# Four staging slots stored from ScalarE's queue, one scatter per four gathers, tile numbers loaded four at a time: a four-layer graph network on one Trainium2 core

## The reference

```python
edge_index = jnp.stack([src, dst])
h = jnp.maximum(_layernorm(x, axis=-1), 0.0)
x = x + _L0_gnn_ref(h, edge_index, ...)      # and in the same way L1, L2, L3

# L0: a message per edge, batch norm over all edges, two segment sums, a two-layer MLP with batch norms
messages = jnp.concatenate([node_rep[src], edge_rep[dst]], axis=-1)
messages = _bn_relu(messages @ W1, g1, b1)
edge_new = jax.ops.segment_sum(messages, dst, num_segments=edge_rep.shape[0])
aggregate = jax.ops.segment_sum(edge_new[dst], src, num_segments=node_rep.shape[0])
h = (1.0 + epsilon) * node_rep + aggregate
out = _bn_relu(_bn_relu(h @ W2a, g2a, b2a) @ W2b, g2b, b2b)
# L1: norm = dinv[row] * edge_weight * dinv[col]; three times
agg = segment_sum(out[row] * norm[:, None], col)
out = out + relu(((1.0 - ALPHA) * agg + ALPHA * x0) @ conv_w[li])
# L2: attention over 4 heads for edge n < 3125, softmax over the heads
# L3: att = sigmoid(a1[row] + a2[col]); out = segment_sum(att[:, None] * x0_j[col], row)
```

## Time and profile before

| | |
|---|---|
| median of three runs | 3692.08 us (3691.84 to 3708.81) |
| the profiled execution | 3690.83 us, its span 3688.8 us |
| mean granted TensorE clock | 0.79 of full speed |
| TensorE (matmuls) / VectorE / ScalarE / GpSimd busy | 69% / 62% / 39% / 30% of the span |
| DMA | 632.29 MB, mean 171 GB/s |
| gather stage, by GpSimd's gathers (L806) | first at 562.0 us, last at 1308.7 us |
| message stage, by VectorE's adds (L1734) | first at 1357.8 us, last at 1751.3 us |
| agg0, by the transposes (L1168) | first at 1785.8 us, last at 2296.6 us |

### The profile page before, as it was taken

How to read it: one execution, slowest core, us unless ns; L and a number is a source line. 1 busy time by engine, 2 the same in 40 slices (tenths; PEclk the granted TensorE clock), 3 DMA queues, 4 the chain that set the end, 5 groups by cost and what they waited for, 6 DMA issues and landing times.

```text
span 3688.8 us, 41851 instructions
## 1 busy us (share of the span) xinstructions
PE 2561.8 (69%) x12402; PEld 2077.5 (56%) x12402; DVE 2288.3 (62%) x4379; ACT 1451.6 (39%) x3050; POOL 1099.4 (30%) x878
## 2 busy tenths in 40 slices
PE   4678714555555536666477777979999999925998
PEld 3522203554555524454366666459888988924786
DVE  4979926888888887877322222354565576626776
ACT  2278813444454410000233333544433434423765
POOL 0016776666666666777200000000000000051000
PEclk9788855555555558888698888979999999967999
DMA  9982225666666655554587777006546645340887
GB/s 373 378 307 27 26 21 155 176 182 184 188 186 188 185 128 141 138 136 105 159 257 230 240 238 216 26 26 185 171 127 172 194 125 169 114 99 8 300 313 265
DMA packets 332245, 632.29 MB, mean 171 GB/s; under 512 B 93155, under 2 KB 206556, under 8 KB 325372
## 3 DMA queue, kind: packets, MB, share of 16 engines
q1 hardware_dynamic: 240350, 550.88, 45.9%
q0 software_dynamic: 78464, 58.39, 10.4%
q10 hardware_dynamic: 13214, 20.35, 1.6%
HBM read 443.97 MB, written 185.52 MB: 171 GB/s over the span
## 4 chain that ended last, share of the span: by engine, by line
PE 31%; DMA 8%; DVE 6%; issue 3%; ACT 3%; SPq 1%; POOL 1%; another core or an unknown queue 0%; DVEq 0%; ACTq 0%
PE banks L1196 25%; DMA weights<-reg 6%; PE banks L1141 2%; DMA ring<-pairs 2%; PE banks L1168 2%; PE banks L1120 1%; ACT reg L996 1%; POOL pairs L798 1%; SPq L712 0%; ACT reg L860 0%; DVE reg L1943 0%; DVE stats L1412 0%; ACT reg L1021 0%; DVE lhs_r L1742 0%; DVE reg L1435 0%
## 5 line engine op out<-in xcount | busy, mean ns | idle before, releaser
L1196 PE MATMUL banks<-rows_r,lhs_r 128*128 128x448 f32 x3850 | 1037.9, 391 | 48.0 <-DVE wts L1853 10.9
L1196 PEld LDWEIGHTS banks<-rows_r,lhs_r 128*128 128x128 f32 x3850 | 756.1, 201 | 135.0 <-DVE att_low L601 23.9
L798 POOL DMA_INDIRECT pairs<-wts x391 | 626.3, 1602 | 501.4 <-DMA weights<-ring 258.5
L1284 PE MATMUL banks<-lhs_r,oT 128*128 x416 | 203.5, 489 | 424.9 <-issue 329.8
L603 DVE SCALAR_TENSOR_TENSOR ring_r<-ring,dinv,rows_r 128x896 fp32r<-128x896 f32 (+1 forms) x300 | 303.4, 1033 | 302.9 <-ACT rows_r L589 302.8
L806 POOL DMA_INDIRECT reg<-tab_p,w x416 | 402.5, 968 | 244.9 <-issue 146.2
L836 POOL DMA_INDIRECT el<-tab_l,base_i x25 | 24.8, 991 | 1481.7 <-DMA tab_l<-reg 1474.4
L589 ACT ACTIVATE rows_r<-ring,dinv 128x896 fp32r<-128x896 f32 (+1 forms) x300 | 284.6, 950 | 393.0 <-PE banks L1196 376.1
L1284 PEld LDWEIGHTS banks<-lhs_r,oT 128*128 128x128 f32 x416 | 132.8, 319 | 437.5 <-issue 437.3
L1323 PE MATMUL banks<-reg 128*128 128x256 f32 x832 | 252.5, 471 | 146.2 <-DVE reg L1734 139.4
L599 DVE TENSOR_TENSOR rows_r<-ring,rows_r 128x448 fp32r<-128x448 f32 x175 | 108.7, 625 | 394.1 <-ACT rows_r L585 394.1
(11 more groups left out here) (256 smaller groups left out, 4432.4 us busy)
## 6 DMA issues: line engine op xcount, KB each, us to landing
ring<-weights SPq DMA_DIRECT2D x225, 448.0 KB, 3.4
ring<-pairs SPq DMA_DIRECT2D x200, 448.0 KB, 4.8
pairs<-ring SPq DMA_DIRECT2D x25, 3136.0 KB, 25.6
ring<-pairs SPq DMA_DIRECT2D x75, 896.0 KB, 5.5
zbuf<-reg SPq DMA_DIRECT2D x208, 256.0 KB
reg<-zbuf SPq DMA_DIRECT2D x52, 1024.0 KB
weights<-reg SPq DMA_DIRECT2D x84, 384.0 KB, 4.8
ring<-weights SPq DMA_DIRECT2D x75, 224.0 KB, 3.3
```

Source lines behind the costliest of these rows:

```text
L798: pool.indirect_dma_start(pairs, bass.IndirectOffsetOnAxis(ap=ix_c[:, k:k + 1], axis=0), vals[:, k, :], None, compute_op=ALU.add).then_inc ...
L1196: m = pe.matmul(bank[:, 0:BLK], lhs[part], rows[:, c:c + BLK], start=first, stop=last)
L1284: m = pe.matmul(ps[4 + q % 2][:, k % 2 * H:(k % 2 + 1) * H], oT[q // 4 % 2][:, k % 8 * P:(k % 8 + 1) * P], part[:, bass.ds(tiles[k], 1), : ...
```

## The change

Three edits:

- **agg0.** `turned` has four slots in place of two; the two new ones lie in the room of `conv` and of `w1`, which are free by then. The stores are issued by ScalarE, one unit after the copy that fills the slot, and no longer by SyncE. The loads of `conv` and of the two attention vectors move behind a wait for all stores.
- **Scatters.** One scatter follows every fourth gather (`C_EVERY = 4`): 104 in the gather stage in place of 52, and 154 after it in place of 206.
- **Tile numbers.** TensorE and VectorE load four with one instruction. TensorE loads the eight of the next pass after the second of its four steps, VectorE where it did before.

```diff
-C_EVERY = 8
-TURN_LAG = 1
+C_EVERY = 4
 TURN_LEAD = 2
+TURN = 4
...
-        turned = [view(RF + k * 8 * P, 4, 2 * P) for k in range(2)]
...
+        turned = [view(RF, 4, 2 * P), view(RF + 8 * P, 4, 2 * P), weight(CONV, 4, 2 * P),
+                  w1_flat.rearrange("p (a b) -> p a b", a=4)]
...
         def turn_slot(q):
-            return pair_no[q] % 2
+            return pair_no[q] % TURN
...
             def stream(pi):
                 if pi == 1:
+                    wait_turned(sp)
+                    sp.dma_start(attn[:, 0, :], attn_l.rearrange("h d -> (h d)").unsqueeze(0).to_broadcast([P, H])).then_inc(gat_loaded, 16)
+                    sp.dma_start(attn[:, 1, :], attn_r.rearrange("h d -> (h d)").unsqueeze(0).to_broadcast([P, H])).then_inc(gat_loaded, 16)
                     sp.dma_start(conv[:, :, :], conv_w.rearrange("l (j p) n -> p (l j) n", p=P)).then_inc(conv_loaded, 16)
-                    wait_turned(sp)
                 for q in range(FIRST[pi] + (RING if pi == 0 else 0), FIRST[pi + 1]):
                     load_unit(q)
-                    if pi == 0 and q >= RING + TURN_LAG:
-                        store_turned(q - RING - TURN_LAG)
-                if pi == 0:
-                    for q in range(FIRST[1] - RING - TURN_LAG, FIRST[1]):
-                        store_turned(q)
...
                 if t % 2 == 0:
-                    wait(act, turn_stored[k], 32 * (pair_no[q] // 2))
+                    wait(act, turn_stored[k], 32 * (pair_no[q] // TURN))
...
+            def store_turned(q):
+
+                _, _, t, (b,) = UNITS[q]
+                if t % 2 == 0 and t < NT - 1:
+                    return
+                k, c0 = turn_slot(q), t // 2 * 2 * P
+                n = min(2 * P, LD - c0)
+                act.wait_ge(drained_a, nth[number["turn", (q,)]])
+                act.dma_start(weights_rows[b * BLK:b * BLK + 3 * P, c0:c0 + n].rearrange("(i p) c -> p i c", p=P),
+                             turned[k][:, 0:3, 0:n]).then_inc(turn_stored[k], 16)
+                act.dma_start(weights_rows[b * BLK + 3 * P:(b + 1) * BLK, c0:c0 + n],
+                             turned[k][0:BLK - 3 * P, 3, 0:n]).then_inc(turn_stored[k], 16)
+
             for q in range(FIRST[1]):
                 if q % ROWS == 0 and q // ROWS < NSPLIT:
                     high_step(0, q // ROWS)
                 high_rows(q)
+                if q > TURN_LEAD:
+                    store_turned(q - TURN_LEAD - 1)
                 if q >= TURN_LEAD:
                     turn_out(q - TURN_LEAD)
...
+            def load_tiles(i):
+
+                for k in range(8 * i, 8 * i + 8, 4):
+                    tiles[k:k + 4] = nc.values_load_multi_w_load_instructions(
+                        tile_ix[0:1, k:k + 4], engines=[pe.engine], min_val=0, max_val=NT - 1)[1]
...
                 if q % 4 == 0:
                     pe.wait_ge(oT_ready, q // 4 + 1)
-                    tiles[2 * q:2 * q + 8] = [pe.value_load(tile_ix[0:1, k:k + 1], min_val=0, max_val=NT - 1) for k in range(2 * q, 2 * q + 8)]
...
                     add_q(q)
+                    if q % 4 == 1 and i + 1 < NPASS:
+                        load_tiles(i + 1)
...
-                tiles = [v.value_load(tile_ix[0:1, k:k + 1], min_val=0, max_val=NT - 1) for k in range(8 * i, 8 * i + 8)]
+                tiles = []
+                for k in range(8 * i, 8 * i + 8, 4):
+                    tiles += nc.values_load_multi_w_load_instructions(
+                        tile_ix[0:1, k:k + 4], engines=[v.engine], min_val=0, max_val=NT - 1)[1]
```

More of the change, by code:

```diff
@@ L393, in gnn_kernel @@
         assert 10 * NCH <= CONV
+        turned = [view(RF, 4, 2 * P), view(RF + 8 * P, 4, 2 * P), weight(CONV, 4, 2 * P),
+                  w1_flat.rearrange("p (a b) -> p a b", a=4)]
+        assert len(turned) == TURN
         ix_c = wts[:, CONV:CONV + NCH].bitcast(I32)
@@ L450, in gnn_kernel @@
         same_ready, same_tot, cells_ready = names("same_ready", "same_tot", "cells_ready")
-        turn_stored = [sem(f"turn_stored{k}") for k in range(2)]
+        turn_stored = [sem(f"turn_stored{k}") for k in range(TURN)]
         pair_full = [sem(f"pair_full{k}") for k in range(RING // 2)]
@@ L540, in turn_slot @@
         def turn_slot(q):
-            return pair_no[q] % 2
+            return pair_no[q] % TURN
         def wait_turned(eng):
-            for k in range(2):
-                eng.wait_ge(turn_stored[k], 32 * len(range(k, n_pairs, 2)))
+            for k in range(TURN):
+                eng.wait_ge(turn_stored[k], 32 * len(range(k, n_pairs, TURN)))
         lhs_r = {at: rounded(f"lhs_r{at // W_}", at, W_) for at in sorted({at for pair in lhs_at for at in pair})}
@@ L702, in load_unit @@
                     sp.dma_start(slot[:, 0:n], weights_rows[t * P:(t + 1) * P, c0:c0 + n]).then_inc(full, 16)
-            def store_turned(q):
-                _, _, t, (b,) = UNITS[q]
-                if t % 2 == 0 and t < NT - 1:
-                    return
-                k, c0 = turn_slot(q), t // 2 * 2 * P
-                n = min(2 * P, LD - c0)
-                sp.wait_ge(drained_a, nth[number["turn", (q,)]])
-                sp.dma_start(weights_rows[b * BLK:b * BLK + 3 * P, c0:c0 + n].rearrange("(i p) c -> p i c", p=P),
-                             turned[k][:, 0:3, 0:n]).then_inc(turn_stored[k], 16)
-                sp.dma_start(weights_rows[b * BLK + 3 * P:(b + 1) * BLK, c0:c0 + n],
-                             turned[k][0:BLK - 3 * P, 3, 0:n]).then_inc(turn_stored[k], 16)
             def stream(pi):
                 if pi == 1:
+                    wait_turned(sp)
+                    sp.dma_start(attn[:, 0, :], attn_l.rearrange("h d -> (h d)").unsqueeze(0).to_broadcast([P, H])).then_inc(gat_loaded, 16)
+                    sp.dma_start(attn[:, 1, :], attn_r.rearrange("h d -> (h d)").unsqueeze(0).to_broadcast([P, H])).then_inc(gat_loaded, 16)
                     sp.dma_start(conv[:, :, :], conv_w.rearrange("l (j p) n -> p (l j) n", p=P)).then_inc(conv_loaded, 16)
-                    wait_turned(sp)
                 for q in range(FIRST[pi] + (RING if pi == 0 else 0), FIRST[pi + 1]):
                     load_unit(q)
-                    if pi == 0 and q >= RING + TURN_LAG:
-                        store_turned(q - RING - TURN_LAG)
-                if pi == 0:
-                    for q in range(FIRST[1] - RING - TURN_LAG, FIRST[1]):
-                        store_turned(q)
             sp.wait_ge(en_added, KS)
@@ L748, in _ @@
                 stream(pi)
-                if pi == 0:
-                    sp.wait_ge(filled, number["Q", (12,)] + 1)
-                    sp.dma_start(attn[:, 0, :], attn_l.rearrange("h d -> (h d)").unsqueeze(0).to_broadcast([P, H])).then_inc(gat_loaded, 16)
-                    sp.dma_start(attn[:, 1, :], attn_r.rearrange("h d -> (h d)").unsqueeze(0).to_broadcast([P, H])).then_inc(gat_loaded, 16)
             for s in range(NSPLIT):
@@ L1005, in _ @@
             for q in range(FIRST[1] - TURN_LEAD, FIRST[1]):
+                store_turned(q - 1)
                 turn_out(q)
+            store_turned(FIRST[1] - 1)
             for stage, dest, nj in (("h2", h2T, 2 * JH), ("h3", h3T, JH)):
```

1 line of the change is left out of this document (added).

## The result

The kernel after the change takes 3462.65 us (median of four runs, 3456.73 to 3465.51), the kernel before 3695.32 us on the same chip (four runs, 3691.84 to 3708.81). The ratio is 0.9362, with a 95% interval of 0.9334 to 0.939: 6.4% faster. The forecast was 3515 us in a range of 3455 to 3590.

The account below looks back on a forecast made before the run. No engine full in the gather stage, VectorE pacing messages, scatters ending last before agg0, store waits in agg0; 0 - 100 + 2 - 81 + 3 = -176 from 3690.8 gives 3515 us, range 3455 to 3590.

Parts of the forecast that it names:

- Better: Rival: GpSimd at 14.0 us a pass (-20) and DMA at a share of 1 (-31), 3464 us; chance 0.13.
- Gather stage, 0 forecast: Gather stage: no change from 52 more scatters and moved tile-number loads, bounds -20 and +100 us.
- so 120 us are left to absorb the 100: Gather stage: GpSimd's 260 us idle, less 140 of DMA gaps, leaves 120 for the added scatters' 100 us.
- scatters stretch the gather stage: Rival: GpSimd's 98.7 us of waits for VectorE stay; price up to 100 us, at 80 3595 us; chance 0.10.
- Message stage, 7.55 to 6.2 us a pass, -70: Message stage: loads of four tile numbers shorten each of 52 passes from 7.55 to 6.2 us, 70 us in all.
- Between the stages, -100, the adds end last: Before agg0: scatters are covered by 20 us, so SyncE's first `pairs` load comes at 1682, not 1781.4: -100 us.
- Start of agg0, +2: Start of agg0: sum of `en` and first split, now uncovered behind the last add, mostly absorbed by slack: +2 us.
- attention vectors, +3: After agg0: the attention vectors wait for the last store's landing, some 3 us, before the next stage: +3 us.
- agg0, -81: agg0: with four slots the store waits go; 486 us become 405 at a DMA share of 0.92: -81 us.
- 0.77 x 486 = 374 us at a share of 1: agg0: DMA's floor, its share of 0.77 over 486 us taken as 374 us at full share.
- the slower rival: Rival: ScalarE's DMA issues block it in agg0 at 2.35 us each, 110 us longer, 3706 us; chance 0.03.
- agg0 keeps its pace: Rival: agg0's wait for stores becomes a wait for loads on shared DMA engines; price 81, 3596 us; chance 0.09.

## Why the prediction was right, and where its sum was off

The direction held, and so did the places of the gain, the message stage and agg0. The sum was -176 us; the profiled executions differ by 225. That the time lies in the range is in part luck: agg0 gave 91 us more than its term and the front of the program 44 us less, and 3463 is 8 us from the lower bound. It is also the 3464 of the rival "Better" (chance 0.13), but not for its reasons: the gather stage didn't shrink by 20 us, it grew, and agg0 gave far more than that rival's 112 us. Of the signs named, the last gather came at 1352, under the bound of 1360 that would have said wrong, but not near 1309; and SyncE's first load stands 16 us behind the last add, not directly behind it. Point by point:

- **Gather stage, 0 forecast, +43 measured (+54 on a second chip).** The bound of +100 was named; the choice of zero failed. The step was "so 120 us are left to absorb the 100". GpSimd absorbed 90 of 209 us when none and 104 were compared, since its waits come while VectorE stands. The other reason, TensorE's loop "is shortened", was true and worth 11 to 15 us; of the stall of 320 us, 221 stayed. So +43 and +54 are net of it, and the scatters alone cost 69 us where 52 more of them were measured. The rival "scatters stretch the gather stage" was right that such waits stay in part (98.7 us before, 51.8 after), and its price of 80 lies nearer to that 69 than zero does.
- **Message stage, 7.55 to 6.2 us a pass, -70.** 5.97 us and -82. The choice near the lower end held: 0.34 us for a load of four. The Trainium skill's figure ("Runtime: NRT & Kernel Launch", Instruction fetch mechanics, about 200 ns for each register even in bulk) stands there for the registers that the runtime loads. It doesn't carry over to this row, which is 0.34 us for four registers and 0.30 for one, so 0.013 us for each further one. The prediction's estimate from it was a pass of 6.8 us; the measured 5.97 decides.
- **Between the stages, -100, the adds end last.** -56. The scatters ended last: the last gather was at 1352.2, the last scatter at 1718.6, 9 us behind the last add. The missing 44 us are the gather stage's 43, passed on to both. Beside that, the order was wrong on its own account: behind the gathers a scatter took 2.37 us and not 2.27 (the step had said that at 2.4 us the scatters would not be covered), and the adds took 12 us less than forecast. So the scatters would have ended last with a last gather at 1308.7 too, and the message stage's extra 12 us gained nothing.
- **Start of agg0, +2; attention vectors, +3.** +2.5, and 175 us in place of 172 for the window behind agg0.
- **agg0, -81.** -172 by the window, -178 by the transposes. This is the mis-sized term. That the waits for stores go was right, and that TensorE and DMA come next too. The size failed at "0.77 x 486 = 374 us at a share of 1". The same 114.6 MB that took a share of 0.77 for 486 us took 1.01 for 314, 317 us. A share is the time in which packets are under way, and before, each stayed under way longer for its bytes: 236 / 0.77 = 306 GB/s, after 366 / 1.01 = 362. The earlier trace rows had the warning in it: while `pairs` was zeroed 404 GB/s went with 1.05, 385 for a share of 1. The second floor taken, TensorE's 360.6 us, fell to 296 with the clock, as "less if it rises" had allowed.
- **ScalarE's issues, the slower rival.** Refuted: 0.37 and 0.52 us at a DMA share of 1.01, near. The single long ones (up to 1.64 us) cost nothing that shows. The row with the 2.35 us was one of SyncE's fifteen weight loads at the stage's start, and no measure for a store on another queue.
- **"agg0 keeps its pace" and the rule of the Trainium skill** ("DMA: Bandwidth & Descriptors", Issuing engines are not separate DMA queues). The runs agree with the rule: four slots on SyncE's queue alone reach 361 GB/s against 366, and 339.5 us of transposes against 333 to 339 with ScalarE's (on other chips). But the conclusion drawn from it, that then the queue adds nothing, held only with four slots. With two, ScalarE's queue gave some 145 to 150 us (366 against 511 and 517 on two chips), by when the stores were issued and not by who carried them. The prediction looked at the 4.8 us of landing and not at the 3.9 us (in the median) before it; this was in the trace, as SyncE's 323.6 us of waits.

What stays open: why the packets took less time for the same bytes at the higher load was not taken apart, and neither what holds TensorE's semaphores back in the gather stage nor how the scatters add to it is known. That the scatters cost 1.15 to 1.35 us each there is shown, by which path is not.

## What to carry to other kernels

- An issuing queue executes in order: a store that stands behind a load which waits for a free place goes out when that place is free, not when its data are ready. Measure a buffer's round trip from the end of the write to the issue and from there to the landing, before more buffers are given to it.
- A stall that has left the line where it was looked for may stand at the next one: TensorE's 310.9 us in front of its steps became 70.1, and 132.3 us in front of the degree count. Add up an engine's stalls over the stage before the gain is booked.
- A DMA share times its time is no floor, and neither is an engine's busy time at a lower clock. Both came down by 15 to 18% once the stall was gone. As a floor take the bytes at the best rate that the same trace shows for such transfers.
- Idle time of an engine isn't free time when it lies where the engine waits for another to free its buffers. Of 209 us of work put into GpSimd's 294 idle us, 119 came out on the stage. It was still a gain, since a scatter costs 1.15 to 1.35 us in the stage and 2.3 to 2.4 behind it.

## What the runs showed of the hardware

- VectorE's TENSOR_LOAD of four registers from a tile takes 0.34 us, of one 0.30 us; on TensorE in the gather stage 0.35 us for four and 0.30 for one.
- One DMA queue was nearly as fast as two: 361 GB/s at a share of 101.2% on q1 alone, 366 GB/s on q1 and q10 together (on another chip).
- GB/s for a share of 1 went from 306 to 362 for the same transfers, as the rate rose from 236 to 366 GB/s, while a store's landing stayed at 4.8 us and a load's rose from 4.8 to 5.3 us.
- In the gather stage TensorE's semaphore updates came up to 11 us behind the recorded end of the matmuls that make them, at times seven at once, and VectorE stood for them 38 times, 136.5 us in all, in the kernel after.
- TensorE's granted clock was 0.85 in agg0 while it had work in 74% of the time and stood still at ScalarE's copies, and 1.00 with work in 94%.
